# Attention layer over a graph of 8192 nodes: x times W as three fp32r products, the range guard moved into the row blocks, both paths in one block

## The reference, cut to what matters

```
Wh = x @ W.T                                  # x [8192, 256], W [256, 256]
s_i = Wh @ r[:256]; s_j = Wh @ r[256:]
e = leaky_relu(s_i[:, None] + s_j[None, :], 0.2)
e = where(adj == 0, -inf, e)                  # adj [8192, 8192] int32
h = gelu(softmax(e, axis=1) @ Wh)             # exact gelu
out = layernorm(x + h)                        # no scale, no shift
```

## Time and profile before

| what | value |
|---|---|
| median of three runs | 1568.44 us |
| the profiled execution's own time | 1567.79 us |
| its span, first to last instruction | 1566.0 us |
| TensorE busy | 1547.4 us, 99% |
| VectorE busy | 1483.5 us, 95% |
| ScalarE busy | 1178.5 us, 75% |
| GpSimd busy | 460.7 us, 29% |
| granted TensorE clock, mean | 0.995 of full speed |
| the cast P_hi (line 460) | 512 of them, 1048 ns each |

### The profile page before, as it was taken

The page is one execution under the profiler, slowest core; times in us unless marked ns, Lnnn a source line. Parts: engine busy times, 40 slices in busy tenths (PEclk is TensorE's granted clock), DMA queues, the critical chain, the costliest instruction groups (busy, mean ns, idle before and its releaser), DMA issues.

```text
span 1566.0 us, 37044 instructions
## 1 busy us (share of the span) xinstructions
PE 1547.4 (99%) x12711; PEld 1535.3 (98%) x12711; DVE 1483.5 (95%) x1851; ACT 1178.5 (75%) x1528; POOL 460.7 (29%) x671
## 2 busy tenths in 40 slices
PE   9999999999999999999999999999999999999995
PEld 8899999999999999999999999999999999999995
DVE  5799999999999999999999999999999999999995
ACT  6767777777777777787777777778777777877773
POOL 1121233333323333322333332233333223333320
PEclk9999999999999999999999999999999999999998
DMA  9636687868588687858877785887777688777760
GB/s 209 121 56 87 92 117 101 113 88 126 73 126 118 101 109 93 121 75 126 115 106 104 97 117 78 128 111 108 102 102 115 80 127 106 105 106 104 108 94 28
DMA packets 295124, 164.16 MB, mean 105 GB/s; under 512 B 12320, under 2 KB 291104, under 8 KB 295072
## 3 DMA queue, kind: packets, MB, share of 16 engines
q0 software_dynamic: 278976, 142.12, 69.5%
q1 hardware_dynamic: 16096, 21.54, 5.0%
HBM read 289.41 MB, written 8.42 MB: 190 GB/s over the span
## 4 chain that ended last, share of the span: by engine, by line
PE 96%; issue 3%; POOL 0%; ACT 0%; DVE 0%; ACTq 0%; POOLq 0%
PE acc L760 31%; PE acc L750 30%; PE acc L753 30%; PE acc L698 3%; PE acc L686 1%; PE acc L720 0%; PE acc L664 0%; ACT P_hi L460 0%; POOL adj_in L257 0%; POOL rstd L310 0%; PE acc L728 0%; ACT Pw L349 0%; POOL rstd L334 0%; ACT gates L367 0%; ACTq L58 0%
## 5 line engine op out<-in xcount | busy, mean ns | idle before, releaser
L750 PE MATMUL acc<-WV_hi,P_hi 128*128 (+1 forms) x4096 | 997.4, 282 | 0.5 <-ACT P_hi L460 0.4
L753 PE MATMUL acc<-WV_lo,P_hi 128*128 (+1 forms) x4096 | 996.7, 281 | 0.0
L750 PEld LDWEIGHTS acc<-WV_hi,P_hi 128*128 128x128 f32 x4096 | 773.7, 189 | 1.1 <-ACT P_hi L460 0.8
L460 ACT CAST P_hi<-Pw 128x1024 fp32r<-128x1024 f32 x512 | 536.3, 1048 | 314.6 <-DVE Pw L576 157.5
L753 PEld LDWEIGHTS acc<-WV_lo,P_hi 128*128 128x128 f32 x4096 | 771.7, 188 | 0.0
L576 DVE SCALAR_TENSOR_TENSOR Pw<-R_row,X,gatesT 128x512 f32<-128x512 f32 x1024 | 709.9, 745 | 0.5 <-issue 0.5
L586 DVE TENSOR_TENSOR P_lo<-Pw,P_hi 128x1024 fp32r<-128x1024 f32 x512 | 624.3, 1219 | 37.8 <-ACT P_hi L460 35.1
L257 POOL DMA_DIRECT2D adj_in<-in_adj x512 | 330.2, 654 | 878.8 <-ACT gates L367 851.4
L760 PE MATMUL acc<-WV_hi,P_lo 128*128 (+1 forms) x4096 | 575.5, 283 | 0.0
L367 ACT ACTIVATE gates<-adj_in 128x1024 uint8<-128x1024 bf16 x512 | 536.8, 1048 | 31.1 <-DMA adj_in<-in_adj 24.6
L760 PEld LDWEIGHTS acc<-WV_hi,P_lo 128*128 128x128 f32 x4096 | 526.7, 189 | 0.0
(11 more groups left out here) (83 smaller groups left out, 221.1 us busy)
## 6 DMA issues: line engine op xcount, KB each, us to landing
adj_in<-in_adj POOLq DMA_DIRECT2D x512, 256.0 KB, 5.3
out<-y SPq DMA_DIRECT2D x64, 128.0 KB, 6.1
y<-in_x POOLq DMA_DIRECT2D x60, 128.0 KB, 6.0
Pw<-in_x SPq DMA_DIRECT2D x48, 128.0 KB, 3.9
R_row<-w_rows SPq DMA_DIRECT2D x15, 256.0 KB, 6.7
x_res<-in_x SPq DMA_DIRECT2D x20, 128.0 KB, 2.8
w_in<-in_L_gnn_W SPq DMA_DIRECT2D x1, 256.0 KB, 2.8
w_rows<-w_in SPq DMA_DIRECT2D x1, 32.0 KB, 2.1
```

Source lines behind the costliest of these rows:

```text
L460: nc.scalar.copy(P_hi[:, u % 2], Pw[u][:]).then_inc(s_hi, 1)
L750: nc.tensor.matmul(acc[r_][:, v, 0:HC], P_hi[:, u % 2, par, bass.ts(v, P)], WV_hi[:, k, :], start=(first and u == 0 and par == 0), stop=False)
L753: nc.tensor.matmul(acc[r_][:, v, 0:FOUT], P_hi[:, u % 2, par, bass.ts(v, P)], WV_lo[:, k, :], start=False, stop=False)
```

## The change

- Prologue: x transposed and W transposed are each kept as an upper part in fp32r and a lower part (the rest). A product is now upper by upper, upper by lower and lower by upper, twelve fp32r calls in a round in place of four fp32 calls. ScalarE's copy makes the upper part, and VectorE makes the lower one (`x_low`). The parts lie in `P_hi` and `P_lo`, which the row blocks use later.
- The maximum of |Wh| for each round, the maxima of |x| and the sums of |W| are gone. In place of them ScalarE sums |WV_hi| over two chunks at a time, 32 times in row blocks 0 and 1 (`wh_size`), then adds these up and takes one Exp, in front of its loop.
- The verdict: GpSimd computes it behind its last adjacency load, TensorE counts the partitions' votes with one small product behind its last product, and VectorE writes the flag after the last reciprocal.
- The end of the prologue is in another order: ScalarE's last copy of x comes ahead of the high parts, VectorE's `copy_s` and low parts of one round come later, and the transpose of line 733 comes behind all late products.
- Both paths are in one block. Each engine does its narrow part, drains, counts up `s_done`, loads the flag, and branches over its general part.

```diff
+        xT_hi = P_hi[:, 1]
+        xT_lo = P_hi[:, 0]
+        w_hi = P_lo[:, 0, :, 0:HC]
+        w_lo = P_lo[:, 1, :, 0:HC]
...
+            def x_low(j):
+                dve.wait_ge(s_xTc, j + 1)
+                nc.vector.tensor_tensor(xT_lo[:, j % 2, :], ps_xT[j % 2], xT_hi_read[:, j % 2, :],
+                                        ALU.subtract).then_inc(s_xTl, 1)
...
             def wh_product(j):
                 pe.wait_ge(s_xTc, j + 1)
+                if j == 0:
+                    pe.wait_ge(s_wTc, KT + 1)
+                    pe.wait_ge(s_wl, KT + 1)
                 if j >= 3:
-                    pe.wait_ge(s_max, j - 2)
+                    pe.wait_ge(s_s, j - 2)
                 for r_ in range(2):
                     for k in range(KT):
-                        last = nc.tensor.matmul(ps_wh[j % 3][:, r_, :], xT[:, j % 2, bass.ts(KT * r_ + k, P)],
-                                                w_ext[:, k, :], start=(k == 0), stop=(k == KT - 1))
+                        nc.tensor.matmul(ps_wh[j % 3][:, r_, :], xT_hi[:, j % 2, bass.ts(KT * r_ + k, P)],
+                                         w_hi[:, k, :], start=(k == 0), stop=False)
+                        nc.tensor.matmul(ps_wh[j % 3][:, r_, :], xT_hi[:, j % 2, bass.ts(KT * r_ + k, P)],
+                                         w_lo[:, k, :], start=False, stop=False)
+                pe.wait_ge(s_xTl, j + 1)
+                for r_ in range(2):
+                    for k in range(KT):
+                        last = nc.tensor.matmul(ps_wh[j % 3][:, r_, :], xT_lo[:, j % 2, bass.ts(KT * r_ + k, P)],
+                                                w_hi[:, k, :], start=False, stop=(k == KT - 1))
                 last.then_inc(s_wh, 1)
...
                             nc.scalar.copy(P_hi[:, u % 2], Pw[u][:]).then_inc(s_hi, 1)
...
+                            if sizes_from is not None and (c > 0 if before is False else c % 2 == 0):
+                                n = sizes_from + (4 * c + u - 4 if before is False else 2 * c + u)
+                                if n < NC // 2 and (before or n < 20):
+                                    wh_size(n)
+                def wh_size(n):
+                    if n == NC // 2 - 2:
+                        act.wait_ge(s_hi0, NC)
+                    act.wait_ge(s_size, n)
+                    nc.scalar.activation(unread[:], WV_hi_read[:, 2 * n:2 * n + 2, 0:FOUT], ACT.Abs,
+                                         accum_out=size[:, n:n + 1]).then_inc(s_size, 1)
+                row_block(0, 0, before=False, sizes_from=0)
+                row_block(0, 1, sizes_from=20)
+                act.wait_ge(s_size, NC // 2)
+                nc.scalar.activation(size[:], size[:], ACT.Identity, accum_out=sizes[:]).then_inc(s_size, 1)
+                nc.scalar.activation(e_M[:], top[:], ACT.Exp, scale=-ALPHA).then_inc(s_size, 1)
                 with act.Fori(1, NAH - 1) as ah:
...
+                pe.wait_ge(s_fit, 7)
+                pe.wait_ge(s_g, RT * (NB + 1))
+                nc.tensor.matmul(ps_votes, fits[:, 2:3], fits[:, 2:4], start=True, stop=True).then_inc(s_vote, 1)
             applies(pe, main)
+            pe.drain().then_inc(s_done, 1)
...
                 nc.vector.reciprocal(rden[:], den[:]).then_inc(s_rden, 1)
+                dve.wait_ge(s_vote, 1)
+                nc.vector.tensor_scalar(taken[0:1, 0:1], ps_votes[:, 0:1], P - 0.5, None, ALU.is_ge).then_inc(s_flag, 1)
...
         def branch(eng, body):
+            flag = eng.value_load(taken[0:1, 0:1], min_val=0, max_val=1)
+            with eng.If(flag == 0):
+                eng.wait_ge(s_done, 5)
                 body()
```

More of the change, by code:

```diff
@@ L249, in _, with on_gpsimd @@
             applies(sp, main)
+            sp.drain().then_inc(s_done, 1)
         NP = NC // 2
-        @block.gpsimd
-        def _(pool):
+        def on_gpsimd(pool):
             def load(ah, r_, cp, i):
@@ L274, in _ @@
             load(0, 0, 1, 1)
[L275 to L289, removed]
+            pool.wait_ge(s_red, 1)
+            nc.gpsimd.partition_all_reduce(top[:], red[:, 0:1], P, REDUCE_MAX).then_inc(s_top, 1)
             def main():
@@ L335, in _, with on_scalar @@
             applies(pool, main)
-        @block.scalar
-        def _(act):
+            pool.drain().then_inc(s_done, 1)
+        def on_scalar(act):
             act.sem_inc(s_g, 2 * RT)
@@ L442, in main, with row_block @@
                 steps = {1: gelu, 3: row_sums, 5: row_squares, 7: scaled}
-                def row_block(ah, r_, before=True, last=False):
+                def row_block(ah, r_, before=True, last=False, sizes_from=None):
                     t = 2 * ah + r_
@@ L480, in _, with on_vector @@
             applies(act, main)
-        @block.vector
-        def _(dve):
+            act.drain().then_inc(s_done, 1)
+        def on_vector(dve):
             nc.vector.memset(zeros, 0.0).then_inc(s_warm, 1)
@@ L599, in piece @@
                         weights(n, r_, cp, i, u, first)
+                        if first and u == 1:
+                            dve.wait_ge(s_wh, NP)
                         if u > 0:
@@ L657, in _, with on_tensor @@
             applies(dve, main)
-        @block.tensor
-        def _(pe):
+            dve.drain().then_inc(s_done, 1)
+        def on_tensor(pe):
             pe.sem_inc(s_free, 2)
@@ L857, in general_path, with on_sync @@
         s_st = sem("out_stored")
-        block = ctx.enter_context(nc.Block())
         def branch(eng, body):
-            if taken is None:
+            flag = eng.value_load(taken[0:1, 0:1], min_val=0, max_val=1)
+            with eng.If(flag == 0):
+                eng.wait_ge(s_done, 5)
                 body()
-            else:
-                flag = eng.value_load(taken[0:1, 0:1], min_val=0, max_val=1)
-                with eng.If(flag == 0):
-                    body()
-        @block.sync
-        def _(sp):
+        def on_sync(sp):
             def body():
@@ L1071, in _ @@
             branch(pe, body)
+        return on_sync, on_gpsimd, on_scalar, on_vector, on_tensor
 def layer(nc, x, adj, W, r, out):
     w_rows = nc.dram_tensor("w_rows", (x.shape[0] // BANK, BANK), F32).ap()
-    with nc.sbuf_tensor("taken", [1, 1], I32) as taken:
-        narrow_path(nc, x, adj, W, r, out, w_rows, taken)
-        general_path(nc, x, adj, W, r, out, taken)
+    with ExitStack() as sems, nc.sbuf_tensor("taken", [1, 1], I32) as taken:
+        s_done = sems.enter_context(nc.semaphore("narrow_part_over"))
+        narrow = narrow_path(nc, sems, x, adj, W, r, out, w_rows, taken, s_done)
+        general = general_path(nc, sems, x, adj, W, r, out, taken, s_done)
+        block = sems.enter_context(nc.Block())
+        @block.sync
+        def _(sp):
+            narrow[0](sp)
+            general[0](sp)
+        @block.gpsimd
+        def _(pool):
+            narrow[1](pool)
+            general[1](pool)
+        @block.scalar
+        def _(act):
+            narrow[2](act)
+            general[2](act)
+        @block.vector
+        def _(dve):
+            narrow[3](dve)
+            general[3](dve)
+        @block.tensor
+        def _(pe):
+            narrow[4](pe)
+            general[4](pe)
 def kernel(**inputs):
```

159 lines of the change are left out of this document (83 added, 76 removed).

## The result

The changed kernel takes 1565.93 us (median of 12 runs, 1564.24 to 1569.43); the kernel before takes 1569.37 in the same session (12 runs, 1567.83 to 1570.69). The ratio is 0.9979 [0.9971, 0.9988]: 3.3 us faster. The forecast was 1556. The profiled executions differ by as much: 1567.79 us before, 1564.46 after (span 1562.7). They divide as follows.

What follows compares the result with a forecast made beforehand. TensorE was taken to bound the kernel; -9.2 + 0.1 + 0.4 + 0.1 + 0.4 - 3.9 = -12.1 us from 1567.79 gave 1555.7, forecast as 1556. The range was 1553.5 to 1561.

Steps and rivals of the forecast that it cites:

- step 4: Row blocks, Exp behind the first Gelus: extra table loads on ScalarE, nearly hidden from TensorE; +0.4 us, between 0.1 and 0.6.
- (1): Prologue rounds of x times W: a round takes 1.88 us instead of 2.19, first product 0.2 us later; together -9.2 us.
- (2): From the last round to row block 0's first product: 9.9 us against 9.54, +0.4; ends -0.8 and +2.9.
- (5): End of the run: one block hides TensorE's branch, leaving SP's own path; 1562.1 instead of 1566.0, -3.9 us.
- rival 1: Prologue rounds held at 2.0 to 2.18 us by ScalarE with its gates or by transfers; 1561 us, chance 0.11.
- nothing waits by these rows: Prologue loads of x and adjacency: they arrive in time at the faster rounds; 1.5 us if the queues grow longer.
- The first sum: Last round to row block 0: TensorE's transposes, products, copy and cast add to 8.7 us if the clock holds.
- third case: Last round to row block 0: if all of it runs at half the clock, about 12.4 us.
- First two row blocks: ScalarE's 32 sums of absolutes, 0.62 us each, are covered by TensorE; 0.1 us charged, 19 us without cover.
- Rival 3: TensorE's outer loop over the row blocks must fetch code at each back jump, 8 x 3.7 = 30 us; 1586, chance 0.04.
- Its ends: Whole run: range 1553.5 to 1561; lower end from bridge and end (-1.2, -0.3) and tables (-0.3), upper from rivals.
- rival 4: Prologue rounds: twelve products at 0.18 us each keep a round at 2.19, and the end stays; 1568, chance 0.03.

Runs made afterwards that it cites:

- e10: e8 with full products in the last two rounds, 22 idle products behind the row product, and the prologue's gates two rounds later; 1555.79 us, ratio 0.9909.
- e8: e6 with the product of r ahead of the first transposes of x and one idle product behind the second transposes; 1561.74 us, ratio 0.9954.
- e7: The kernel after with 45 empty instructions (drains) at the start of ScalarE's code; 1569.89 us, ratio 1.0014.
- e3: The kernel after with its two paths in two blocks again; 1569.04 us, ratio 0.9998.
- e4: The kernel after with full 258-column products in the last two rounds, in place of two-column and late products; 1564.24 us, ratio 0.9962.
- e2: The kernel after without ScalarE's 32 sums of absolutes, `size` filled with ones; 1570.56 us, ratio 1.0005.
- e1: The kernel after with the Exp that makes e_M moved back into the prologue; 1597.1 us, ratio 1.0165.
- e6: e1 with ten more empty instructions (drains) at the start of ScalarE's code; 1560.9 us, ratio 0.995.
- e12: The kernel before with its two paths in one block, nothing else; 1566.54 us, ratio 0.9973.

## Why the prediction was wrong

The sign was right and the size was not: 12.1 forecast, 3.3 measured. The 8.8 that are missing: 3.1 in the row blocks (step 4), 2.9 in the rounds (1), 2.0 in the bridge (2), 0.8 at the end (5). By its own steps:

1. **Rounds of x times W: right in the rate, mis-sized by 2.9 us.** 1.89 us for 1.88; neither ScalarE with its gates nor the transfers held it up in the rounds (rival 1 falls), and in e10, with another start and later gates, the last full round ends at 65.05 where the forecast had 64.2 and the kernel after 67.17. What was missing: the first product 0.8 us late, 1.7 us of clock, and 29 rounds 0.01 longer, together 2.8 of the 2.9. "I put its start 0.2 us later" counted the new low parts by their lengths. The product of r, its copy and its low part now stand between the first transposes and the first product, in a row, and x itself landed at 6.75. e8 put the product at 8.17 by moving them. That the clock would fall here was not considered at all: before, it did not, nor did it in the trace of e7, whose code differs by ScalarE's padding alone. The gates were closer to waiting than the prediction had it ("nothing waits by these rows"): in e8, where the rounds begin 0.85 us earlier, the first one stood 2.5 us for its load.
2. **The bridge: +2.4 for +0.4.** The first sum was right: 8.7 us if the clock holds, and e3's trace, where it held, has 9.0 (the two-column products take 2.7 us, where it had 3.0). The failed choice was "if it falls for as long as it does now (3.4 us)": it fell for 6.8, and all late products ran at half rate. My own third case, 12.4, was the one that came; 11.9 was measured. I took 9.9 as the value between, although the text itself said that the two-column stretch was now longer. What decides whether the clock falls there stays open: it fell in the kernel after and not in e3, with the same code up to there, and it fell without any two-column product in e4.
3. **First two row blocks: right.** A sum costs 0.63 us start to end and its read 0.19; blocks 0 and 1 don't change without them (e2). Cover was TensorE, as said.
4. **The Exp after the Gelu: the largest failed step**, 3.6 us for the 0.4 and 0.1 given to the row blocks. Both counts and price were off. I counted one load for each turn; there are two, since the set at the loop's entry (Exp's) is not the one at its end (Gelu's), so the head loads one too. And I priced each at the 0.09 us of the one load in the earlier trace rows, which stood in the middle of a row block's slack. At the loop's head a turn costs 0.36, and the entry, two loads in a row, 1.3. I had argued that "nothing in that stretch speaks for" more; it could not, as it held no such place. e1's blocks 1, 2 and 10 and all of e6 show the cost gone with the loads.
The 0.8 missing are stores that landed later: 4.3 us behind their issue in both kernels with a single block (after, e12), 3.4 to 3.5 in the two others. Whether that is because the other engines now fetch their last code beside them (q14's packets at 1559.44 and 1559.90) is argued, not tried. Votes, verdict and GpSimd's operations cost nothing: VectorE's wait for the first Gelu is 0.58 us where the earlier trace rows had 0.61.
6. **Rival 3 was the right mechanism in the wrong place.** TensorE's loop had no such wait. ScalarE's has one in the kernel before, hidden; the change moved the loop into three packets by accident and so took it away. e1, whose loop begins one instruction earlier, was 26 us slower than the kernel before by the ratio (28 by the medians). That this is close to the 30 at which the rival was priced is chance: those were eight stalls of 3.7 us on TensorE, these are five of 4.4 to 5.2 us and the clock behind them.
   The Trainium skill, Runtime: NRT & Kernel Launch, section Instruction fetch mechanics, gives blocks of 16 KiB, 256 instructions, and two resident ones. q8's packets are of that size, and ScalarE's (q14) are of half of it. With two blocks of 256 on ScalarE a loop of 342 to 344 instructions would be fetched again only where it touches three blocks, and wherever their boundaries lie, that cannot be so for both 377 to 718 (before) and 491 to 834 (e7). Both fetch at every back jump, so here the measurement decides.

Two sums of the prediction don't come out as written. Its ends add up to 1556 - 1.2 - 0.3 - 0.3 = 1554.2, where the range begins at 1553.5. And rival 4's 0.18 us a product makes a round of 0.44 + 12 x 0.18 = 2.6 us, not 2.19, which takes 0.146. Neither touches the forecast.

Open: what decides whether the clock falls in the bridge, and why stores land later with a single block.

## What to carry to other kernels

Before moving an activation, list ScalarE's function sets in order around its loops: a different set at entry and exit costs a load at the loop's head in every turn, in front of whatever stands first there. Price a stall at the place where it will stand, not by the mildest row of its kind. And when code ahead of a loop changes, count where the loop falls: ten empty instructions were worth 34 us here.

## What the runs showed of the hardware

- A loop of 342 to 344 instructions on ScalarE ran without fetches when it touched three packets of 8192 bytes (117 to 129 instructions each by the positions, taken as 128), and waited at each of five back jumps when it touched four: 1.1 to 1.3 us each in the mean, and 6.5 to 7.2 in e1, where the first packet held a single instruction of the loop. The second packet of a fetch began 4.9 to 6.2 us behind the first.
- A product in fp32r with 2 moving columns costs 0.112 us, one with 258 columns 0.119: small products save next to nothing.
- A table load takes 1.283 us each time, 15 times in one kernel, with no further gap before or behind it.
- The granted clock went from 1.00 to 0.50 in the first rounds, in the bridge, and after stalls of 2.35 us (e8) and 4.4 us (e1), and stayed there for 3.4 or 6.8 us. Each of these followed a stretch with waits or two-column products. With the same code it fell in the bridge of the kernel after and not in that of e3, 2.9 us apart; before and e12 are another such pair, 1.6 us apart.
- The clock doesn't explain why the runs of the kernel after scatter by 5 us: its four fastest (1564.24 to 1564.58) all have a mean of 0.993, and one of 1567.39 has 0.996. What some traces have besides is a gate that stands for a late adjacency load: 3.7 us in e4, whose row block 7 took 92.99 us, and 3.3 in e10, whose block 4 took 92.64.
